# Four graph layers in one kernel: three TensorE transposes replaced by VectorE block transposes and DMA through a scratch in HBM

## The reference

```
x = layernorm(x + max_n relu(A[o,n] + (C-A)[o,m]))         # layer 0, A = adj @ x, C = adj @ x + b
h = x @ W                                                   # layer 1, one attention over the nodes
att = softmax(leaky_relu(s1[i] + s2[j]) * adj, axis=j);  s1, s2 = h @ a1, h @ a2
x = layernorm(x + elu(att @ h + beta * h))
x = layernorm(x + (adj @ x) @ weight + bias)                # layer 2
q, k, v = x@Wq+bq, x@Wk+bk, x@Wv+bv  (8 heads of 64)        # layer 3
w = softmax(q k^T / 8 + (adj == 0 ? -1e9 : 0), axis=keys)
x = layernorm(x + w @ v)
```

## Time and profile before

| | |
|---|---|
| median of 3 runs | 2746.28 us (2746.2 to 2747.28) |
| the profiled execution | 2746.01 us |
| its span, first to last instruction | 2744.2 us |
| TensorE, matmuls | 2677.5 us busy, 98% |
| VectorE | 1925.9 us, 70% |
| ScalarE | 1474.4 us, 54% |
| GpSimd | 1483.6 us, 54% |
| DMA | 75.19 MB in 41607 packets, 27 GB/s on average |
| mean granted TensorE clock | 0.993 of full speed |

### The profile page before, as it was taken

One profiled execution on the slowest core, in us unless ns is written; L12 is line 12 of the kernel. 1 busy time (PEld: TensorE's weight loads), 2 busy tenths in 40 slices (PEclk: granted clock), 3 DMA queues, 4 the chain that ended last, 5 costly groups with the idle time before them and its releaser, 6 DMA issues.

```text
span 2744.2 us, 60531 instructions
## 1 busy us (share of the span) xinstructions
PE 2677.5 (98%) x19593; PEld 2404.0 (88%) x19593; DVE 1925.9 (70%) x6165; ACT 1474.4 (54%) x4360; POOL 1483.6 (54%) x1806
## 2 busy tenths in 40 slices
PE   4899999999999999999999999999999999999996
PEld 3799899889889889989988988988998998898896
DVE  7777776776777776777767767767777777767753
ACT  3355555555555555555555555555555555555554
POOL 5655555555555555555555555555556555555541
PEclk9999999999999999999999999999999999999998
DMA  4000000000000000000000000000000000000000
GB/s 124 15 22 28 28 24 27 27 24 27 24 27 27 19 29 30 20 27 31 19 27 31 20 27 31 20 27 31 20 27 27 24 27 27 24 27 27 13 16 24
DMA packets 41607, 75.19 MB, mean 27 GB/s; under 512 B 5584, under 2 KB 5712, under 8 KB 41424
## 3 DMA queue, kind: packets, MB, share of 16 engines
q1 hardware_dynamic: 41424, 73.49, 8.3%
HBM read 39.92 MB, written 33.55 MB: 27 GB/s over the span
## 4 chain that ended last, share of the span: by engine, by line
PE 96%; DVE 1%; issue 1%; ACT 1%; DMA 0%; POOL 0%; ACTq 0%; SPq 0%; POOLq 0%; DVEq 0%
PE rot L796 24%; PE rot L798 23%; PE rot L797 23%; PE score L917 5%; PE rot L904 5%; PE rot L853 4%; PE rot L889 4%; PE rot L939 2%; PE rot L952 2%; PE rot L873 2%; PE rot L877 2%; PE s_bank L861 0%; PE att_bank L945 0%; DMA probs<-in_L_gnn_W 0%; DVE x L644 0%
## 5 line engine op out<-in xcount | busy, mean ns | idle before, releaser
L338 POOL TENSOR_TENSOR ve<-mv,eps_col 128x1 f32<-128x1 f32 (+1 forms) x448 | 88.1, 197 | 695.5 <-ACT e L503 352.8
L796 PE MATMUL rot<-w_hi,y_hi 128*128 128x512 f32 x1024 | 425.2, 415 | 5.6 <-DVE y_lo L634 4.7
L360 POOL TENSOR_TENSOR x2b<-x,bias 128x512 f32<-128x512 f32 x128 | 203.5, 1590 | 416.4 <-DVE x L644 416.4
L798 PE MATMUL rot<-w_hi,y_lo 128*128 128x512 f32 x1024 | 404.8, 395 | 0.0
L797 PE MATMUL rot<-w_lo,y_hi 128*128 128x512 f32 x1024 | 404.2, 395 | 0.0
L549 ACT ACTIVATE probs<-score,sc_nmax 128x128 f32<-128x128 f32 x1024 | 357.0, 371 | 11.4 <-DVE sc_nmax L757 11.4
L796 PE MATMUL rot<-xt_hi,wk_hi 128*128 128x256 f32 x1024 | 299.8, 293 | 0.0
L634 DVE TENSOR_TENSOR y_lo<-rot,y_hi 128x512 fp32r<-128x512 f32 x128 | 88.5, 691 | 296.4 <-ACT y_hi L467 296.4
L798 PE MATMUL rot<-xt_hi,wk_lo 128*128 128x256 f32 x1024 | 290.2, 283 | 0.0
L798 PE MATMUL rot<-xt_hi,wq_lo 128*128 128x256 f32 x1024 | 289.8, 283 | 0.0
L797 PE MATMUL rot<-xt_lo,wq_hi 128*128 128x256 f32 x1024 | 289.7, 283 | 0.0
(11 more groups left out here) (117 smaller groups left out, 7758.5 us busy)
## 6 DMA issues: line engine op xcount, KB each, us to landing
x_in<-in_x SPq DMA_DIRECT2D x128, 256.0 KB, 2.6
out_x<-x SPq DMA_DIRECT2D x128, 256.0 KB, 2.2
probs<-in_L_gnn_W SPq DMA_DIRECT2D x1, 1024.0 KB, 8.0
v_sb<-in_L_gnn_weight SPq DMA_DIRECT2D x1, 1024.0 KB, 7.1
probs<-in_L_gnn_Wv SPq DMA_DIRECT2D x1, 1024.0 KB, 5.4
v_sb<-in_L_gnn_Wq SPq DMA_DIRECT2D x1, 1024.0 KB, 5.3
probs<-in_L_gnn_Wk SPq DMA_DIRECT2D x1, 1024.0 KB, 5.4
x<-in_L_gnn_a SPq DMA_DIRECT2D x1, 512.0 KB, 5.7
```

Source lines behind the costliest of these rows:

```text
L360: pool.tensor_tensor(x2b[:, :], x2[:, slot.buf(L_GCN, 2), :], bias2[:, :], ALU.add)\
L796: pe.matmul(outp, lh, rh, start=first, stop=False)
L798: return pe.matmul(outp, ll, rh, start=False, stop=last)
```

## The change

The three groups of transposes of layer 3 are no longer done by TensorE with an identity matrix. VectorE's `transpose` turns each 32 x 32 block of a tile in its place; the blocks are then put where they belong by DMAs: for each of the four bands of 32 partitions one DMA (`scatter`) writes them to a scratch in HBM, 32 floats (128 B) at a time, and when all four have landed, one DMA (`gather`) reads the tiles back with 512 B per row. All of them are issued by SyncE.

- Probabilities: VectorE's transpose of all 8 tiles (1024 elements per partition) into `probs_b`, which takes the place of the second buffer of `probs`, stands first in its slot. Then four scatters and a gather into `probs_t`. The exps of the scores always write the first buffer and wait for that transpose.
- x3: `x3_b` right behind x3 on VectorE, four scatters, a gather into the new `xt_f`; xt_hi and xt_lo read `xt_f` instead of PSUM.
- PV result: the copy `o_t` becomes a block transpose; four scatters, a gather into `o_norm`, in which the multiplication by the reciprocals is then done in place. This multiplication and GpSimd's addition of `o_norm` come one slot later (`L_ON` = `L_PV` + 1). The statistics of the last norm move on VectorE from the head of the slot to behind the attention weights, and their aggregation behind the reciprocal of the row sums; GpSimd's rounding remainder of x (`low_x`) is issued before the addition of `bv`.
- The waits for `rot[2]`, `rot[0]` and `rot[3]` on TensorE are those for the jobs that are left in these banks.

The core of the diff:

```diff
+            def scatter(hbm, blocks, landed):
+                for a in range(P // BLOCK):
+                    rows = slice(a * BLOCK, (a + 1) * BLOCK)
+                    sp.dma_start(hbm.rearrange("n (b r) p -> r (n b) p", r=BLOCK)[:, :, rows],
+                                 blocks[rows, :].rearrange("r (m c) -> r m c", c=BLOCK)).then_inc(landed, 16)
+            def gather(tiles, hbm, landed):
+                sp.dma_start(tiles, hbm.rearrange("n q p -> q n p")).then_inc(landed, 16)
...
             def emit(slot):                      # SyncE
+                if slot.on(L_PV):
+                    slot.wait(sp, probs_b_done, L_PV)
+                    scatter(pt_hbm, probs_b, pt_scattered)
+                if slot.on(L_TR):
+                    slot.wait(sp, x3_b_done, L_TR)
+                    scatter(xt_hbm, x3_b, xt_scattered)
+                if slot.on(L_PV):
+                    slot.wait(sp, pt_scattered, L_PV, each=SCATTER)
+                    gather(probs_t[:, :, :, :].rearrange("p c t n -> p (c t) n"), pt_hbm, pt_in)
+                if slot.on(L_TR):
+                    slot.wait(sp, xt_scattered, L_TR, each=SCATTER)
+                    gather(xt_f[:, :, :], xt_hbm, xt_in)
                 if slot.on(L_LOAD):
...
                                      x4[:, first + g, :]).then_inc(out_stored[g], 16)
+                if slot.on(L_PV):
+                    slot.wait(sp, x4_done, L_PV, 1)
+                    slot.wait(sp, o_t_done, L_PV)
+                    scatter(ot_hbm, o_t, ot_scattered)
+                    slot.wait(sp, ot_scattered, L_PV, each=SCATTER)
+                    gather(o_norm[:, :, :].rearrange("p g (c e) -> p (g c) e", e=P), ot_hbm, ot_in)
...
             def emit(slot):                      # VectorE
+                if slot.on(L_PV):
+                    slot.wait(dve, score_exp, L_PV)
+                    slot.wait(dve, pt_scattered, L_PV, 1, SCATTER)
+                    dve.transpose(probs_b[:, :], probs[:, 0, :, :, :].rearrange("p c t n -> p (c t n)"))\
+                        .then_inc(probs_b_done, 1)
...
+                    slot.wait(dve, x3_done, L_TR)
+                    slot.wait(dve, xt_scattered, L_TR, 1, SCATTER)
+                    dve.transpose(x3_b[:, :], x3[:, c2, :]).then_inc(x3_b_done, 1)
+                if slot.on(L_ON):
+                    slot.wait(dve, ot_in, L_ON, each=16)
+                    slot.wait(dve, inv_done, L_ON)
+                    heads = o_norm[:, :, :].rearrange("p g (c d) -> p (g c) d", d=HEAD)
+                    dve.tensor_tensor(heads, heads,
+                                      sc_inv[:, :].unsqueeze(2).to_broadcast([P, CHUNKS * TILES, HEAD]),
+                                      ALU.mult).then_inc(o_norm_done, 1)
...
-                    slot.wait(dve, ot_mm, L_PV, 1)
-                    dve.tensor_copy(o_t[:, :], rot[3][:, :]).then_inc(o_t_done, 1)
+                    slot.wait(dve, ot_scattered, L_PV, 1, SCATTER)
+                    dve.transpose(o_t[:, :], rot[3][:, :]).then_inc(o_t_done, 1)
...
             # ScalarE
-                    slot.wait(act, xt_mm, L_TR)
+                    slot.wait(act, xt_in, L_TR, each=16)
...
             # TensorE
-                    for t in range(TILES):
-                        ins = pe.transpose(rot[3][:, t * P:(t + 1) * P], probs[:, par, 0, t, :], ident[:, :])
-                    ins.then_inc(pt0_mm, 1)
...
-                    for t in range(TILES):
-                        ins = pe.transpose(rot[0][:, t * P:(t + 1) * P], probs[:, par, 1, t, :], ident[:, :])
-                    ins.then_inc(pt1_mm, 1)
...
-                    slot.wait(pe, pt0_done, L_PV)
-                    slot.wait(pe, pt1_done, L_PV)
+                    slot.wait(pe, pt_in, L_PV, each=16)
+                    slot.wait_last(pe, (v_done, L_V, 1), (o_t_done, L_PV, 1))
...
-                    for n in range(GROUP * CHUNKS):
-                        ins = pe.transpose(rot[3][:, n * P:(n + 1) * P], o_t[:, n * P:(n + 1) * P], ident[:, :])
-                    ins.then_inc(ot_mm, 1)
...
-                    for k in range(KC):
-                        ins = pe.transpose(rot[2][:, k * P:(k + 1) * P], x3[:, slot.buf(L_TR, 2), k * P:(k + 1) * P],
-                                           ident[:, :])
-                    ins.then_inc(xt_mm, 1)
```

More of the change, by code:

```diff
@@ L361, in emit @@
                         .then_inc(x2b_done, 1)
+                if slot.on(L_ON):
+                    k, first = slot.part(L_ON), slot.buf(L_ON, BUFS) // GROUP * GROUP
+                    slot.wait(pool, o_norm_done, L_ON)
+                    if k == 0:
+                        slot.wait(pool, x4_init, L_ON - (GROUP - 1))
+                    res = x4[:, first:first + GROUP, k * CHUNKS * P:(k + 1) * CHUNKS * P]
+                    pool.tensor_tensor(res, res, o_norm[:, :, :], ALU.add).then_inc(x4_done, 1)
                 if slot.on(L_OUT) and slot.part(L_OUT) == GROUP - 1:
@@ L394, in emit @@
                         .then_inc(r1_sum_done, 1)
+                low_x(Slot(slot.base, slot.offset + 1))
                 if slot.on(L_V):
@@ L402, in emit @@
                                        bv_row[:, :], ALU.add).then_inc(x4_init, 1)
-                if slot.on(L_PV):
-                    k, first = slot.part(L_PV), slot.buf(L_PV, BUFS) // GROUP * GROUP
-                    slot.wait(pool, o_norm_done, L_PV)
-                    if k == 0:
-                        slot.wait(pool, x4_init, L_PV - (GROUP - 1))
-                    res = x4[:, first:first + GROUP, k * CHUNKS * P:(k + 1) * CHUNKS * P]
-                    pool.tensor_tensor(res, res, o_norm[:, :, :], ALU.add).then_inc(x4_done, 1)
-                low_x(Slot(slot.base, slot.offset + 1))
                 if slot.on(L_GAT):
@@ L539, in emit @@
                     par = slot.buf(L_QK, 2)
-                    slot.wait(act, pt1_mm, L_QK, 2)
+                    slot.wait(act, probs_b_done, L_QK, 1)
                     slot.wait(act, inv_done, L_QK, 2)
@@ L622, in emit @@
             def emit(slot):
-                last = slot.on(L_OUT) and slot.part(L_OUT) == GROUP - 1
-                if last:
-                    first = slot.buf(L_OUT, BUFS) // GROUP * GROUP
-                    slot.wait(dve, x4_done, L_OUT)
-                    for g in range(GROUP):
-                        statistics("3", x4[:, first + g, :], g)
-                    slot.wait(dve, st_done["3"], L_OUT)
+                if slot.on(L_PV):
[3 more added lines that the diff above has]
+                        .then_inc(probs_b_done, 1)
+                last = slot.on(L_OUT) and slot.part(L_OUT) == GROUP - 1
                 if slot.on(L_GAT):
@@ L635, in emit @@
                         .then_inc(y1_lo_done, 1)
-                if last:
-                    aggregate("3", 0, GROUP)
                 if slot.on(L_GCN):
@@ L649, in emit @@
                     slot.wait(dve, rs_done["2"], L_TR)
-                    slot.wait(dve, xt_mm, L_TR, 2)
                     slot.wait(dve, x4_init, L_TR, 2)
@@ L690, in emit @@
                                              op0=ALU.mult, op1=ALU.add).then_inc(att_n_done, 1)
+                if last:
+                    first = slot.buf(L_OUT, BUFS) // GROUP * GROUP
+                    slot.wait(dve, x4_done, L_OUT)
+                    for g in range(GROUP):
+                        statistics("3", x4[:, first + g, :], g)
+                    slot.wait(dve, st_done["3"], L_OUT)
                 if slot.on(L_PV):
```

82 lines of the change are left out of this document (36 added, 46 removed).

## The result

| | before | after |
|---|---|---|
| median | 2746.64 us (4 runs) | 3111.06 us (3105.22 to 3111.98, 4 runs) |
| ratio | | 1.1322, 95% interval 1.1302 to 1.1342 |
| span profiled | 2744.2 us | 3108.7 us |
| mean granted clock | 0.993 | 0.926 |

The account below looks back on a forecast made before the run. TensorE, busy 98%, was taken as the bound. Counted from a PV start, 12.8 to first packet, 0.384 us per ns of packet price (20 ns), 1.7 gather packets and 0.85 landing give 23.05; 112.0 + 127 x 23.05 = 3039 us, range 2730 to 4000.

Parts of the forecast that it names:

- the price of a packet: Scratch writes by DMA: 20 ns per 128 B packet, so the probabilities' packets run from 12.8 to 17.9 after PV start.
- What is removed: TensorE: four groups of four transposes leave, 1.58 us a slot; with everything added hidden, the slot would be 19.16.
- The forecast 11.9: SyncE: first scatter of the probabilities issued 11.9 us after PV start, VectorE's block transpose being done at 11.8.
- my lower bound: 128 B scratch write: at least 13.4 ns a packet, as cheap as a read on a line between measured sizes.
- rival 2: SyncE's queue: order of issues, not packets, decides; slot 20.7, 2741 us give or take 60; chance 0.12.
- The estimate of 27 ns: 128 B scratch write: 13.4 ns doubled for a read-modify-write, for which the sum gives 3376 us.
- the estimate of 8 ns: 128 B scratch write: about three DMA cycles a packet over its 32 B beats, leaving queue order as the limit.
- The issues: SyncE: 15 scatter and gather issues added each slot at 0.4 us; x3's four run from 15.6 to 17.2.
- The gather: Probabilities' read back: 27 ns per 512 B packet, packets from 20.5 to 22.2 behind x3's, landed at 23.05.
- rival 4: TensorE: idling drops the clock to 1.2 GHz; a third gives slot 25, 3290 us, all 29, 3790; chance 0.14.
- Cover: Transfers off the loop: PV result has 7 us of cover, x3's gather 2.6; last norm ends about 22, covered at 23.
- What would show it: Profile signs: TensorE 85% busy, PV waits 3 to 5 us; against: no PV wait, issues much over 0.5, clock under 0.95.

Follow-up runs that it names:

- 12: Kernel before with only x3's transposes moved to VectorE blocks and DMA; probabilities and PV result stay on TensorE: 2694.68 us, ratio 0.9813.
- 4: Changed kernel with the probabilities' eight transposes back on TensorE and their copies on ScalarE; x3 and PV result by DMA: 2909.97 us, ratio 1.0595.
- 9: Changed kernel with the probabilities' gather ahead of x3's scatters and the last norm's output later on ScalarE, no filler: 2889.84 us, ratio 1.0523.
- 10: Changed kernel with probabilities' gather first, last norm's output later on ScalarE, and 10 unused TensorE transposes ahead of PV's wait: 2832.85 us, ratio 1.0316.
- Experiment 2: Changed kernel with the probabilities' wait and gather issued ahead of x3's wait and scatters on SyncE: 2962.84 us, ratio 1.0786.
- experiment 1: Changed kernel plus 24 unused transposes of the identity on TensorE ahead of the PV matmuls' wait: 2964.88 us, ratio 1.0797.
- 3: Changed kernel with x3's transposes back on TensorE; probabilities and PV result still by DMA: 3014.71 us, ratio 1.0966.
- 5: Kernel with probabilities on TensorE, x3 and PV result by DMA, and the last norm's output behind y2_hi and att_t on ScalarE: 2806.62 us, ratio 1.0223.

## Why the prediction was right, and where it was not

The sign, the size and the place were right: 3111 lies in 2730 to 4000, near the likeliest, and TensorE waits for the gather of the probabilities before PV. But the 23.05 was a sum in which a term far too large stood for three that were missing, so that it came within 0.6 us of the slot was in part luck. The step that failed in it is the price of a packet. Step by step:

- **What is removed.** 1.58 us a slot of transposes: x3's part was given as 0.36 and is 0.40 (12). With no wait left TensorE's floor shows: the shortest slots of 4 are 19.87, where eight transposes (0.79) are back, which leaves 19.08 for the forecast 19.16.
- **Block transposes.** 1.21 us for 1024 elements (forecast 1.3), 0.71 for 512. Right.
- **xt_lo, costed at nothing: missed, without effect on this time.** It takes 1.42 us instead of 0.68. In the changed kernel it has 0.1% of the chain, since the slot is closed by way of x3_b. With the gather first it is in the loop (3.9% of the chain in 9) and costs the 0.57 of 10. The forecast 11.9 for the first issue then has 0.25 left that I did not trace: 12.15 in the short slots of 10, at full clock.
- **The price of a packet: the step that failed.** I took 20 ns for 128 B. In 1538.00 to 1539.00, where the short writes of x3 run, 113 GB/s at a share of 0.66 are 16 x 0.66 x 128 / 113 = 12 ns; that is a little under my lower bound of 13.4. So 5.1 us for the scatter's packets shrink to 3.1, and rival 2 had the mechanism: the queue's order decides. Experiment 2 shows it. With rival 2's sum, 20.65 as its terms add up, the terms that were missing are 1.5 for the clock, 0.4 for the issues and 1.3 for the gather: 23.85. The estimate of 27 ns that I had hung on the Trainium skill, "DMA: Bandwidth & Descriptors", Specifications, is not borne out; the estimate of 8 ns from the same page of the Trainium skill, section Why small descriptors are slow, was nearer, though low.
- **The issues.** 0.56 us for each of the probabilities' four, 0.49 for x3's, forecast 0.4: 0.4 more for x3's four.
- **The gather.** Forecast 0.9 + 1.7 + 0.85 = 3.45 behind its issue; 4.73 in the changed kernel, 4.2 with nothing of x3 ahead of it (9). The price of its packets was about right: from 1541.0 to 1541.5, 348 GB/s at a share of 1.15 are 27 ns for 512 B. How much of the 0.8 to 1.3 us missed is fixed time, and how much the packets of other transfers in between, these runs can't tell.
- **The clock: rival 4, beside the forecast and not in place of it.** I gave a third of its effect T = 25. It costs 1.5 us in the slot shown, 1.15 by experiment 1. The rule of the Trainium skill that I had named ("TensorE: Matmul & The Clock Gate", Part 1) agrees with the trace: 0.50 granted behind 3.3 us without work in the changed kernel, 1.00 behind 0.51 in 1.
- **The sum put right.** 11.9 + 0.25 + 0.57 + 1.5 for the first issue (14.2; measured 14.32), which does not close the slot; x3's first issue 1.5 for the clock behind the forecast 15.6 (17.1; 17.24); four issues 1.98; the gather 4.73: 23.8, against 23.95. The average of 23.62 means that other slots were somewhat shorter.
- **Cover.** PV's result over the scratch never stopped TensorE in the changed kernel, and ScalarE's xt_hi was covered, as said. The last norm, "about 22, close but covered at T = 23", was rightly placed: as soon as the slot falls below 23 it is in the way. In 4 it makes every second slot long, and moving its output took 103 us off 4 and 73 off 2. Part of the 73 is not the norm's own: in half the slots of 9 GpSimd's x_lo has moved behind xt_lo, which by 0.57 a slot is an estimated 36 us.
- **What would show it.** Busy share 85% (about 85), packets 1.38 million (1.3), 3.1 us of wait in each of 128 slots (3 to 5): right. The scatter of the probabilities landed 2.7 us behind its issue and not 6: wrong, with the price of a packet. Of the signs I had named against myself one came, a granted clock under 0.95 (0.926); the issues, at 0.49 to 0.56, stand at the edge of another.
- **Slips in the working.** By its own terms the scatter lands ahead of x3_b (15.5) only up to 8 ns a packet; the 15 ns of rival 2 are for landing ahead of the end of x3's issues (17.2), which is what that sum needs. And half of its 0.12 is 0.06, not 0.04. Neither changes the forecast.

Open: what orders the slots of 3 in fours; why the turn of the loop takes VectorE so long; and how much of the gather's 4.2 us is fixed. A version of 12 with the PV result by DMA as well was not run; by 4 and 5 the last norm would have to be moved for it.

## What to carry to other kernels

A transpose through a scratch in HBM is a wait of 8.6 us from the first scatter's issue to the gather's landing (4.4 + 4.2 here), for 0.8 us of TensorE. It pays where the result has a whole slot of slack, as x3 has, and not where the consumer stands in the loop that starts it. Before taking work off a full engine, follow each removed job to its reader and ask what is in the loop then: TensorE, when it gets a wait of some us, also pays with its clock; an instruction of VectorE whose operands both lie in SBUF can take twice as long beside one of GpSimd; and of several transfers in one queue the one with a reader in the loop goes first. And where a change has three parts, time them apart: here the one without a deadline gave 1.9% by itself, and together with either of the others the kernel was slower than before.

## What was not expected of the hardware

- xt_lo, a float32 subtraction of 128 x 512 on VectorE, takes 0.68 us with one operand in PSUM, also while GpSimd works (before: 0.69 at most, in all 128). With both operands in SBUF it takes 0.68 where GpSimd has not started ahead of it and 1.42 where GpSimd's x_lo has (the rows in 9 and 10). It was 1.42 in nearly all slots of the changed kernel and in half of those of 9, so that it is not the place of the operands alone. o_norm, with both operands in SBUF, takes 0.65 to 0.70 while GpSimd is idle, 0.94 in the other slots of the changed kernel and 1.78 in 119 of 128 in 3. No run moved GpSimd's work for this by itself.
- 128 B writes to HBM go at 12 ns a packet and engine (1538.0 to 1539.0 of the changed kernel).
- The length of the wait ahead of PV does not tell by itself whether the clock falls. In 2 it fell behind 1.94 to 2.61 us without work in 46 slots of 90, and stayed at 1.00 behind 1.80 to 2.56 in the other 44; in 5 it fell behind 2.14. In 2 the slot that begins behind 2.49 us is 22.87 long, the one behind 2.30 is 21.46. 24 useless matmuls (2.8 us) took 146 us off the time.
- A DMA of many short runs holds SyncE 0.49 to 0.56 us for its issue, a load or a gather of 256 KB 0.36 to 0.38 us.
